# Two experts of eight in a four-block network: the first layer with the weights as the stationary side

## The reference

```python
logits = flat @ router_w.T                       # flat: 2048 tokens x 192
probs = softmax(logits)
topk_probs, topk_idx = top_k(probs, 2)
balanced = topk_probs / balance[topk_idx]        # balance: from the mean use of each expert
balanced = balanced / balanced.sum(-1)
h = silu(einsum('th,eih->tei', flat, w1))        # w1: 8 experts, 512 x 192
outs = einsum('tei,ehi->teh', h, w2)             # w2: 8 experts, 192 x 512
combined = (take(outs, topk_idx) * balanced).sum(1)
```

## Time and profile before

| | |
|---|---|
| median of 3 runs | 1185.02 us (1184.45 to 1185.32) |
| the profiled execution | 1190.96 us |
| its span, first to last instruction | 1188.8 us |
| PE busy | 1011.8 us, 85% of the span |
| PEld busy | 766.9 us, 65% |
| DVE busy | 576.6 us, 49% |
| ACT busy | 423.8 us, 36% |
| POOL busy | 291.6 us, 25% |
| mean granted TensorE clock | 0.898 |

### The profile page before, as it was taken

How to read it: one execution, slowest core, us unless ns; L and a number is a source line. 1 busy time by engine, 2 the same in 40 slices (tenths; PEclk the granted TensorE clock), 3 DMA queues, 4 the chain that set the end, 5 groups by cost and what they waited for, 6 DMA issues and landing times. The chain is left out here.

```text
span 1188.8 us, 20456 instructions
## 1 busy us (share of the span) xinstructions
PE 1011.8 (85%) x7507; PEld 766.9 (65%) x7508; DVE 576.6 (49%) x1395; ACT 423.8 (36%) x858; POOL 291.6 (25%) x399
## 2 busy tenths in 40 slices
PE   6796899999699698999799379999397999864696
PEld 5596778787366586788798246666375455562575
DVE  4643555652320575455657634444475777332131
ACT  4554155555322241344351111111055466511232
POOL 4454320110110122000002035554222202105422
PEclk9875899999899899899898589999789999956798
DMA  7443763320012120100009111111234432055610
GB/s 89 115 126 103 164 154 79 100 58 3 1 54 66 39 39 2 54 1 1 2 2 265 37 37 53 48 48 46 62 113 114 127 103 82 2 206 183 249 41 14
DMA packets 103831, 91.60 MB, mean 77 GB/s; under 512 B 26402, under 2 KB 95608, under 8 KB 103103
## 3 DMA queue, kind: packets, MB, share of 16 engines
q1 hardware_dynamic: 90953, 75.58, 23.5%
q0 software_dynamic: 6144, 11.08, 3.5%
q10 hardware_dynamic: 6645, 3.75, 1.1%
HBM read 64.44 MB, written 29.70 MB: 79 GB/s over the span
## 5 line engine op out<-in xcount | busy, mean ns | idle before, releaser
L1224 DVE TENSOR_REDUCE l0a_nmax<-l0a_psS 98x2 f32<-98x392 f32 x96 | 54.4, 567 | 54.5 <-PE l0a_psS L1039 50.5
L868 DVE TENSOR_REDUCE l3a_nmax<-l3a_psS 128x2 f32<-128x512 f32 x96 | 62.0, 686 | 31.6 <-PE l3a_psS L722 31.3
L2627 ACT ACTIVATE l2e_H<-l2e_psH 128x512 f32<-128x512 f32 x40 | 21.7, 594 | 130.0 <-PE l2e_psH L2589 130.0
L824 ACT ACTIVATE l3a_PT<-l3a_psST 128x512 f32<-128x512 f32 x96 | 54.6, 596 | 29.0 <-PE l3a_psST L752 28.5
L1174 ACT ACTIVATE l0a_PT<-l0a_psST 98x392 f32<-98x392 f32 x96 | 47.2, 497 | 42.2 <-PE l0a_psST L1081 41.8
L2607 PEld LDWEIGHTS l2e_psY<-W2T,l2e_HT 128*128 128x128 f32 x320 | 51.5, 190 | 16.3 <-issue 16.2
L2550 POOL DMA_INDIRECT ys<-l2e_Y,result_of x40 | 42.0, 1051 | 72.3 <-DVE l2e_Y L2654 66.2
L2607 PE MATMUL l2e_psY<-W2T,l2e_HT 128*128 x320 | 57.3, 332 | 1.6 <-DVE l2e_Y L2654 0.8
L2545 POOL DMA_INDIRECT l2e_X<-xn,token_at x40 | 39.3, 982 | 38.7 <-PEq L2568 26.9
L2586 PE MATMUL l2e_psH<-W1T,l2e_XT 128*128 x80 | 41.3, 640 | 2.8 <-issue 2.0
L2654 DVE COPY l2e_Y<-l2e_psY 128x384 f32<-128x384 f32 x20 | 11.2, 558 | 65.2 <-PE l2e_psY L2607 60.3
(11 more groups left out here) (552 smaller groups left out, 2712.1 us busy)
## 6 DMA issues: line engine op xcount, KB each, us to landing
l3w_A<-in_w SPq DMA_DIRECT2D x8, 771.0 KB, 12.4
l3w_B<-in_w SPq DMA_DIRECT2D x8, 672.0 KB, 13.4
l3a_QS<-qd SPq DMA_DIRECT2D x72, 64.0 KB, 2.3
l3a_KS<-kd SPq DMA_DIRECT2D x72, 64.0 KB, 2.3
rd<-l0q_r_p SPq DMA_DIRECT2D x24, 168.0 KB
l0a_QS<-qd SPq DMA_DIRECT2D x54, 64.0 KB
l0a_KS<-kd SPq DMA_DIRECT2D x54, 64.0 KB
W2T<-in_w2t SPq DMA_DIRECT2D x2, 1536.0 KB
```

The lines of the kernel that those rows point to most:

```text
L824: nc.scalar.activation(PT[n % 3][:, s, :], psST[item % 2][:, :], ACT.Exp).then_inc(exp_done, 1)
L868: nc.vector.tensor_reduce(nmax[k % 2][:, TI * u:TI * (u + 1), s], psS[item % 2][:, :].rearrange("p (t k) -> p t k", t=TI), AX.X, ALU.max, ...
L1224: mx = nc.vector.tensor_reduce(nmax[k % 2][0:WQ, 2 * j:2 * (j + 1), s], psS[item % 2][0:WQ, 0:2 * W0].rearrange("p (t k) -> p t k", t=2), ...
```

## The change

The first layer's operands change places. The expert's weights become the stationary side, 128 inner channels at a time, and the 128 tokens of the tile the moving one, so that psH has inner channels on partitions and tokens along them. That is the layout that the second layer wants, and Silu writes it straight into HT. `turn_hidden`, psT, H, `hidden_of` and the two semaphores between them go.

The weights of both layers' 192 input channels are now read at fixed places: `turned` copies the expert's 128-channel part too, into W1S (two copies of 128 x 512 a pair), beside the two copies to W1R. PE's `first_layer` loads no expert numbers any more; it waits for the copies first and then does, for each of four blocks of inner channels, two products over 128 channels and two over 64. The pipeline is one step shorter: a slot turns the tokens two pairs ahead, does the first layer of the next pair and the second layer of the current one, in this order. ACT does Silu of the next pair and waits until HT is free; DVE turns first and copies the result after it.

```diff
-        H = [[st.sb(f"H{b}{t}", [P, FI]) for t in range(2)] for b in range(2)]
+        W1S = [[st.sb(f"W1S{b}{t}", [P, FI]) for t in range(2)] for b in range(2)]
...
-        psT = [st.ps(f"psT{t}") for t in range(2)]
...
             def first_layer(q, s):
                 p, b = q * RING + s, s % 2
-                experts = [expert_of(pe, p * 2 + t) for t in range(2)]
                 pe.wait_ge(xt_done, p + 2)
+                pe.wait_ge(w_done, p + 1)
                 pe.wait_ge(h_done, p * 2 + 2)
-                for t, e in enumerate(experts):
-                    nc.tensor.matmul(psH[b][t][:, :], XT[b][:, t, :], W1T[:, 0, bass.ds(e * FI, FI)], start=True, stop=False)
-                pe.wait_ge(w_done, p + 1)
-                for t in range(2):
-                    nc.tensor.matmul(psH[b][t][:, :], XT[b][halves[t], 2, :], W1R[b][halves[t], :], start=False, stop=True).then_inc(h_mm, 1)
-
-            def turn_hidden(q, s):
-                p, b = q * RING + s, s % 2
-                for t in range(2):
-                    pe.wait_ge(h_done, p * 2 + t + 5)
-                    pe.wait_ge(ht_done, p * 2 + t + 1)
-                    for mb in range(NM):
-                        mm = nc.tensor.transpose(psT[t][:, mb * P:(mb + 1) * P], H[b][t][:, mb * P:(mb + 1) * P], G["ident"][:, :])
-                    mm.then_inc(ht_mm, 1)
+                for mb in range(NM):
+                    block_of = slice(mb * P, (mb + 1) * P)
+                    for t in range(2):
+                        nc.tensor.matmul(psH[b][t][:, block_of], W1S[b][t][:, block_of], XT[b][:, t, :], start=True, stop=False)
+                    for t in range(2):
+                        mm = nc.tensor.matmul(psH[b][t][:, block_of], W1R[b][halves[t], block_of], XT[b][halves[t], 2, :], start=False, stop=True)
+                        if mb == NM - 1:
+                            mm.then_inc(h_mm, 1)
...
             def slot(q, s, has):
-                for ahead, step in ((1, turn_hidden), (2, first_layer), (0, second_layer), (3, turn_tokens)):
+                for ahead, step in ((2, turn_tokens), (1, first_layer), (0, second_layer)):
                     if has(ahead):
                         step(q, s + ahead)
...
+                    act.wait_ge(y_mm, p + 1)
                     for t in range(2):
                         act.wait_ge(h_mm, p * 2 + t + 5)
-                        act.wait_ge(ht_mm, p * 2 + t + 1)
-                        nc.scalar.activation(H[b][t][:, :], psH[b][t][:, :], ACT.Silu).then_inc(h_done, 1)
+                        nc.scalar.activation(HT[b][t][:, :, :], psH[b][t][:, :].rearrange("p (m n) -> p m n", m=NM), ACT.Silu).then_inc(h_done, 1)
...
                 for t in range(2):
                     e = expert_of(dve, p * 2 + t)
+                    nc.vector.tensor_copy(W1S[b][t][:, :], W1T[:, 0, bass.ds(e * FI, FI)])
                     cp = nc.vector.tensor_copy(W1R[b][halves[t], :], W1T[halves[t], 1, bass.ds(e * FI, FI)])
                 cp.then_inc(w_done, 1)
-
-            def hidden_of(q, s):
-                p, b = q * RING + s, s % 2
-                dve.wait_ge(y_mm, p + 1)
-                for t in range(2):
-                    dve.wait_ge(ht_mm, p * 2 + t + 5)
-                    nc.vector.tensor_copy(HT[b][t][:, :, :], psT[t][:, :].rearrange("p (m n) -> p m n", m=NM)).then_inc(ht_done, 1)
...
             def slot(q, s, has):
-                if has(1):
-                    hidden_of(q, s + 1)
+                if has(2):
+                    turned(q, s + 2)
                 if has(0):
                     result_of(q, s)
-                if has(3):
-                    turned(q, s + 3)
```

More of the change, by code:

```diff
@@ L2516, in experts_any @@
         psH = [[st.ps(f"psH{b}{t}") for t in range(2)] for b in range(2)]
-        psT = [st.ps(f"psT{t}") for t in range(2)]
         x_in = [st.sem(f"x_in{r}") for r in range(RING)]
         y_out = rows_out
-        xt_mm, xt_done, w_done, h_mm, h_done, ht_mm, ht_done, y_mm, y_done, y_free = st.sems("xt_mm xt_done w_done h_mm h_done ht_mm ht_done y_mm y_done y_free")
+        xt_mm, xt_done, w_done, h_mm, h_done, y_mm, y_done, y_free = st.sems("xt_mm xt_done w_done h_mm h_done y_mm y_done y_free")
         Pb, *M = G["choice"]
@@ L2566, in _ @@
         def _(pe):
-            for sem, k in ((xt_mm, RING), (xt_done, 1), (h_mm, 4), (h_done, 4), (ht_mm, 4), (ht_done, 2), (y_mm, 2), (y_done, 2)):
+            for sem, k in ((xt_mm, RING), (xt_done, 1), (h_mm, 4), (h_done, 4), (y_mm, 2), (y_done, 2)):
                 pe.sem_inc(sem, k)
@@ L2604, in second_layer @@
                 for t, e in enumerate(experts):
-                    pe.wait_ge(ht_done, p * 2 + t + 3)
+                    pe.wait_ge(h_done, p * 2 + t + 5)
                     for mb in range(NM):
@@ L2620, in slot @@
             def slot(q, s, has):
-                if has(2):
-                    s += 2
+                if has(1):
+                    s += 1
                     p, b = q * RING + s, s % 2
+                    act.wait_ge(y_mm, p + 1)
                     for t in range(2):
                         act.wait_ge(h_mm, p * 2 + t + 5)
-                        act.wait_ge(ht_mm, p * 2 + t + 1)
-                        nc.scalar.activation(H[b][t][:, :], psH[b][t][:, :], ACT.Silu).then_inc(h_done, 1)
+                        nc.scalar.activation(HT[b][t][:, :, :], psH[b][t][:, :].rearrange("p (m n) -> p m n", m=NM), ACT.Silu).then_inc(h_done, 1)
             slots_of_pairs(act, slot)
```

## The result

The changed kernel took **1197.11 us** (median of 4 runs, 1195.61 to 1200.36) against 1184.74 (4 runs, 1184.18 to 1185.32) of the kernel before, run beside it: a ratio of 1.0113 [1.0098, 1.0129], slower by 1.1%. Two more comparisons gave 1.0092 [1.0057, 1.0127] and 1.0080 [1.0067, 1.0094]. The forecast was 1193, in 1185 to 1200.

A forecast was written before the change was run, and what follows sets the result against it. PE's own work was taken to bound the two-expert stage. Slots cost 2.6 to 3 us and the half-clock start 5 to 5.5, together +8: span 1188.8 to 1196.8, median 1193, range 1185 to 1200.

The forecast's parts named there:

- Unit of the first layer: Two-expert stage, PE: four 128-row and four 64-row matmuls on one block take 1.05 us, four units 4.20 a slot.
- price of a change of height: PE, first layer: stepping between 128-row and 64-row weights costs 0.20 us whatever the columns; eight changes replace two, +1.2 us.
- rival of nearly free changes: First layer: changes of height cost next to nothing at 128 columns; -27 us, 1158; chance 0.10.
- Slot: Steady two-expert stage: one pair's slot takes 7.69 us against 7.54, +2.6 us over 17 slots.
- Sequencer: PE's register loads of expert numbers in the two-expert stage: the 0.08 us a slot put down to them goes.
- rival of a sequencer that falls behind: Second layer's register loads queue behind 64 more instructions; 0.5 us a slot gives +10, 1203; chance 0.11, shared with later clock rise.
- Copies of W1S: DVE: two more weight copies a slot, 0.42 us each, covered except for the first pair, whose weights come 2.1 us later.
- Clock at the start: Two-expert stage's start: clock stays at half until pair 0's second layer; first layers 7.2 us each; 5 to 5.5 us lost.
- row that stayed down: Recorded stretch with PE always busy on 112-column float32 matmuls, clock at 0.50 through 6.3 us; likened to the new first layer.
- forecast at 0.47: Likeliest case: clock stays at half until pair 0's second layer; 1193 us, chance 0.47.
- Sum: Last second layer starts at 849.5 instead of 841.58: +8 us, 2.6 to 3 from slots, 5 to 5.5 from the start.
- Clock down in the slots: Rival: every first layer runs at half clock, 3.0 us more a slot, +60 over 20 slots, 1253 with the start; chance 0.05.

The follow-up runs named there:

- grouped order: Changed kernel with all 128-row first-layer matmuls before all 64-row ones: 1178.76 us, ratio 0.9949; with expert numbers also loaded at the slot's start, 1165.84 us.
- padded one: Changed kernel, order of matmuls kept, with 64-row weights padded to 128 rows with zeros: 1174.23 us, ratio 0.9919 to the kernel before.
- runs with the clock up: Unused identity products put ahead of and behind first token turnings: changed kernel 1185.4 us, ratio 1.0014; kernel before 1185.83 us, ratio 1.0004.

## Why the prediction was right

The direction, the place and both causes of the loss were right: the changes of height, and the low clock at the start. Two terms were somewhat small, and the reason given for the clock holds only in part.

- *Unit of the first layer*: 1.05 forecast, 1.06 measured, four units 4.25 against 4.20. The price of a change of height, taken from matmuls of 256 and 512 columns, holds at 128. (The 0.2 from 747.05 to 747.25, which the prediction also names, holds a matmul of 0.11 and speaks for 0.09 only.) The rival of nearly free changes is out; its 1158 needs changes taken away, and taking six of eight away (with the loads early) gave 1165.84.
- *Slot*: 7.736 against 7.69. The rest of the miss, 0.05 by 17, is 0.8 us.
- *Sequencer*: its 0.08 went, as taken; the rival of a sequencer that falls behind didn't come. That was nearer than the prediction has it: not 4 us of first layer cover the register loads, but its last 30 loads and matmuls, 2.1 us for 1.7 of register work. The grouped order, with 1.1 there, brings the wait out.
- *Copies of W1S*: 0.41 to 0.43 against 0.42, hidden but for the first pair; its first layer began 4.42 us after the first tokens (4.36 forecast).
- *Clock at the start*: 0.50 forecast through both first layers, and so it was; the clock was back 23.7 us after the first tokens against 24.3 (711.0 less 686.74). The first layers took 7.5 in place of 7.2, a unit at half clock being 1.88, just over the 1.72 to 1.87; the second layer of pair 0 took 4.07 against 4.0. That is 0.7 us of start.
- *The reason for it*: the prediction likened the new first layer, short matmuls with pauses between them, to the row that stayed down. That matmuls are short is not the reason: in the grouped order the same matmuls of 128 columns had the clock back 9.9 us after the first tokens, and in the padded one after 8.2. What the three kernels differ in is the changes of height. So the forecast at 0.47 came true partly by luck. Why the clock stays down under the changes isn't shown.
- *Sum*: the last second layer began 9.5 us later, counted from the first tokens, against +8; the 0.8 of slots and 0.7 of start make up the difference. The split differs a little from the forecast's 2.6 to 3 and 5 to 5.5: by the runs with the clock up it is 3.2 to 3.7 and 5.5 to 6.0.
- *Clock down in the slots*: it was 1.00 in all of the 131.51 us. The Trainium skill (TensorE: Matmul & The Clock Gate, Why this matters for your kernels) warns that the clock swings under thin matmuls in loops that wait for data; here no slot shows it, with a second layer of 2.70 us in each. At the start, ahead of the first second layer, the clock did stay down.
- *Off by 4 us in the whole*: 1.5 of it is the two terms above. The stage is 9.2 us longer in each of three profiles, while the three comparisons give +12.4, +10.9 and +9.5 us (the later two by their ratios). Other stages differ by several us between profiles of one kernel, so scatter may be the rest; that isn't shown.

## What to carry to other kernels

Count, beside columns and instructions, how often consecutive matmuls change the number of weight rows: here each change cost 0.2 us at full clock, as much as two matmuls of 128 columns, so that removing eight transposes lost against six more changes. Sort matmuls by height, or pad the short ones with zeros, and then look for what the longer matmuls had hidden: here register loads in PE's own queue, which had to be moved to the start of the slot. Where a stage begins at half clock, ask of its first operations whether the clock rose under such work anywhere in the trace, and price them at half if it didn't. Compare the order of the matmuls too, not their columns alone: here the order decided.

## What the runs showed of the hardware

- Weight loads between 128-row float32 matmuls are covered, down to 128 columns (32 in a series 0.112 apart), and so are those between 64-row ones of the two halves of the array (16 in 1.09 us). The load after a change between 128 and 64 rows is not, and a change costs 0.20 us at 128, 256 and 512 columns. The Trainium skill (TensorE: Matmul & The Clock Gate, The mechanism) says that loads overlap running matmuls only where the group of rows differs, and in the same section that a load into a background weight buffer is pulled ahead too. The halves agree with the first. The 128-row series, all on the same rows, goes against its "only", and the measurement decides; whether its loads go by way of such a buffer no run here shows.
- PE stayed at 0.50 for 16.46 us in which the profile shows it busy all the time, with changes of height all through. The same matmuls sorted, 16 like ones in a series, had it at 1.00 within one first layer. The first layers of the change, once at 1.00, were kept there. A series of one height isn't enough by itself: under 96-row weights PE was busy for 6.30 us at 0.50.
- Two register loads in PE's queue take 0.6 us, and with the register operations around them the second layer began 1.7 us after the first of these. PE's sequencer came to them when 28 to 30 loads and matmuls were still to start, so they show as soon as the last of the work in front of them is short.
